# Subtracting the softmax row maxima with 32-row matmuls, fed by one turning matmul, in a fused attention and expert layer

## The reference

```python
mask = jnp.abs(idx[:, None] - idx[None, :]) <= half          # half = 32
scores = jnp.einsum('bhqd,bhkd->bhqk', Q, K) / SCALE
scores = jnp.where(mask[None, None], scores, -jnp.inf)
attn = jax.nn.softmax(scores, axis=-1)
out = jnp.einsum('bhqk,bhkd->bhqd', attn, V)
...
x = x + ga * attention(h)
h = layernorm(x) * (1 + cb) + sb
x = x + gb * experts(h)
```

## Time and profile before

| | |
|---|---|
| median of 3 runs | 164.77 us (163.94 to 164.79) |
| the profiled execution | 163.83 us, of which span 162.0 us |
| TensorE busy | 151.1 us, 93% |
| VectorE busy | 127.1 us, 78% |
| ScalarE busy | 90.2 us, 56% |
| GpSimd busy | 55.9 us, 34% |
| TensorE clock granted | 1.0 of full |
| HBM | 3.81 MB read, 2.10 MB written, mean 36 GB/s |

### The profile page before, as it was taken

One profiled execution on the slowest core, in us unless ns is written; L12 is line 12 of the kernel. 1 busy time (PEld: TensorE's weight loads), 2 busy tenths in 40 slices (PEclk: granted clock), 3 DMA queues, 4 the chain that ended last, 5 costly groups with the idle time before them and its releaser, 6 DMA issues.

```text
span 162.0 us, 5111 instructions
## 1 busy us (share of the span) xinstructions
PE 151.1 (93%) x1976; PEld 123.2 (76%) x1976; DVE 127.1 (78%) x353; ACT 90.2 (56%) x172; POOL 55.9 (34%) x109
## 2 busy tenths in 40 slices
PE   6799989999899999999999999999999999888993
PEld 2376778787677898978887888789888986674773
DVE  3439496495988999897999789877988898587872
ACT  3234387556666656575747764785166428624740
POOL 6420072021540606521662147212251306426340
PEclk9999999999999999999999999999999999999999
DMA  4874134034103503510351013401250000010002
GB/s 134 239 210 28 8 38 32 4 65 28 10 0 46 59 0 67 37 34 4 65 33 35 0 35 43 32 0 35 34 36 0 9 28 0 6 32 0 0 4 65
DMA packets 47431, 6.23 MB, mean 38 GB/s; under 512 B 42416, under 2 KB 47024, under 8 KB 47408
## 3 DMA queue, kind: packets, MB, share of 16 engines
q1 hardware_dynamic: 47264, 5.90, 23.4%
q10 hardware_dynamic: 144, 0.00, 0.0%
HBM read 3.81 MB, written 2.10 MB: 36 GB/s over the span
## 4 chain that ended last, share of the span: by engine, by line
PE 71%; issue 9%; ACT 8%; DVE 6%; POOL 4%; POOLq 0%; ACTq 0%; DVEq 0%
PE ps L763 11%; PE ps L797 11%; PE ps L863 10%; PE ps L778 5%; PE ps L856 5%; PE ps L921 3%; PE ps L839 3%; ACT probs L533 3%; PE ps L841 3%; PE ps L840 3%; PE ps L718 3%; PE ps L808 2%; PE ps L740 2%; PE ps L745 2%; PE ps L890 2%
## 5 line engine op out<-in xcount | busy, mean ns | idle before, releaser
L1160 DVE TRANSPOSE_TENSOR_REDUCE blkmax<-ps 128x44 f32<-128x1408 f32 x16 | 26.4, 1648 | 11.7 <-PE ps L770 9.5
L797 PEld LDWEIGHTS ps<-probs,v_bd 128*36 128x36 f32 x640 | 21.5, 113 | 7.4 <-issue 4.7
L533 ACT ACTIVATE probs<-ps 128x704 f32<-128x704 f32 x32 | 23.0, 755 | 6.1 <-PE ps L778 5.6
L797 PE MATMUL ps<-probs,v_bd 128*36 128x96 f32 (+2 forms) x640 | 25.1, 228 | 0.8 <-ACT probs L533 0.5
L359 POOL TENSOR_TENSOR act_w<-act,cw 128x512 f32<-128x512 f32 x15 | 15.7, 1044 | 21.7 <-issue 13.7
L763 PEld LDWEIGHTS ps<-q_sb,k_bd 32*128 32x128 f32 x640 | 19.3, 186 | 4.3 <-issue 2.4
L763 PE MATMUL ps<-q_sb,k_bd 32*128 32x96 f32 (+2 forms) x640 | 21.3, 274 | 0.7 <-ACT probs L533 0.5
L778 PE MATMUL ps<-shift,quad_ones 128*128 128x384 f32 x64 | 16.9, 370 | 0.0
L863 PE MATMUL ps<-wd_sb,act_t 128*128 128x128 f32 x128 | 16.2, 280 | 0.6
L863 PEld LDWEIGHTS ps<-wd_sb,act_t 128*128 128x128 f32 x128 | 15.0, 191 | 2.0 <-ACT act_t L557 1.8
L546 ACT ACTIVATE tanh_g<-ps 128x512 f32<-128x512 f32 x14 | 8.3, 596 | 14.4 <-PE ps L841 14.4
(11 more groups left out here) (108 smaller groups left out, 283.5 us busy)
## 6 DMA issues: line engine op xcount, KB each, us to landing
x_sb<-x SPq DMA_DIRECT2D x8, 128.0 KB, 3.2
v_spill<-v_sb SPq DMA_DIRECT2D x8, 128.0 KB, 2.3
v_bd<-v_spill SPq DMA_DIRECT2D x32, 32.0 KB, 3.1
out<-out_sb SPq DMA_DIRECT2D x7, 128.0 KB, 2.0
wgu_sb<-w_gu SPq DMA_DIRECT2D x1, 512.0 KB, 4.3
wm_sb<-wmod SPq DMA_DIRECT2D x1, 256.0 KB, 3.8
wd_sb<-w_down SPq DMA_DIRECT2D x1, 256.0 KB, 5.2
con<-consts SPq DMA_DIRECT2D x1, 244.0 KB, 3.2
```

Source lines behind the costliest of these rows:

```text
L533: nc.scalar.activation(probs[:, t, hgs, cols], ps[:, hgs, cols], ACT.Exp, scale=float(DH) ** -0.5).then_inc(probs_ready, 1)
L797: last = nc.tensor.matmul(ps[p0:p0 + VW, OB, c0 + lo * KB:c0 + (hi + 1) * KB], v_bd[:, i % VB, kb, hg, :], view(probs[:, t, hg, at:at + 1] ...
L1160: nc.vector.tensor_reduce(blkmax[:, t, :, live(t):live(t) + LIVE], view(ps[:, 0, live(t) * KB:live(t) * KB + 1], [[BANK, NHG], [KB, LIVE], ...
```

## The change

`shift_rows` for two head groups at a time is replaced by three operations for all four head groups of a half. `spread_max` (VectorE) writes `max_by_head`, in which a column stands for one head group, head and query block, and is nonzero only on the partitions of that head. `turn_max` (TensorE) multiplies it as stationary tile by stacked 32x32 identities and puts the sums into 32 free columns of PSUM bank 0, with head group, head and query block on the partition (`hg*KB + g*QBT + qb`, 16 of each 32 in use) and the query along the columns. `shift_rows` (VectorE) multiplies those by `C_QB`, a negative selector of the query block, into `shift`, 128 partitions x 128 columns. `subtract_max` then contracts over the 32 rows of one head group, with `head_ones`. The subtraction is still four matmuls of 384 columns for a half; each now reads 32 rows, not 128. Both pairs wait for the one shift. The turn and the spread are put at places in the hand-written orders; nothing else is moved.

```diff
-    c[:, C_NI:C_NI + KB] = np.where(r[:, None] == q[None], -1.0, 0.0)
-    c[:, C_ONES:C_ONES + 128] = g[:, None] == g[None]
+    c[:, C_ONES:C_ONES + 128] = (r // QBT)[:, None] == g[None]
...
+    c[:, C_QB:C_QB + QBT] = np.where((r % QBT)[:, None] == np.arange(QBT)[None], -1.0, 0.0)
...
+            def turn_max(i, t):
+                wait(pe, spread_ready, i, QT, t + 1)
+                nc.tensor.matmul(ps[:, 0, CELLS * KB:(CELLS + 1) * KB], max_by_head[:].rearrange("p h m -> p (h m)"),
+                                 con[:, C_REP:C_REP + KB], start=False, stop=True, skip_group_check=True)\
+                  .then_inc(turned_ps, 1)
+
             def subtract_max(i, t, pair):
-                wait(pe, shift_ready, i, PARTS, t * NPAIR + pair + 1)
+                wait(pe, shift_ready, i, QT, t + 1)
                 for hg in range(pair * PAIR, (pair + 1) * PAIR):
-                    last = nc.tensor.matmul(ps[:, hg, 0:CELLS * KB], quad_ones[:],
-                                            view(shift[:, hg, 0:1], [[0, 3], [1, QBT * KB]]),
+                    rows = slice(hg * KB, (hg + 1) * KB)
+                    last = nc.tensor.matmul(ps[:, hg, 0:CELLS * KB], head_ones[rows],
+                                            view(shift[rows, 0, 0:1], [[0, 3], [1, QBT * KB]]),
                                             start=False, stop=True, skip_group_check=True)
...
-            def shift_rows(i, t, pair):
+            def spread_max(i, t):
 
                 wait(dve, rowmax_ready, i, QT, t + 1)
+                wait(dve, turned_ps, i, QT, t)
...
+                nc.vector.tensor_tensor(
+                    view(max_by_head[:, 0, 0:1], [[KB, NHG], [QBT, G], [1, QBT]]),
+                    view(row_max[:, 0, 0:1], [[QBT, NHG], [0, G], [1, QBT]]),
+                    view(con[:, C_DEN:C_DEN + 1], [[0, NHG], [1, G], [0, QBT]]), ALU.mult).then_inc(spread_ready, 1)
+
+            def shift_rows(i, t):
+
+                wait(dve, turned_ps, i, QT, t + 1)
                 wait(dve, shifted_ps, i, PARTS, t * NPAIR)
                 nc.vector.tensor_tensor(
-                    shift[:, pair * PAIR:(pair + 1) * PAIR].rearrange("p h (q k) -> p (h q) k", k=KB),
-                    view(row_max[:, pair * PAIR, 0:1], [[1, PAIR * QBT], [0, KB]]),
-                    view(con[:, C_NI:C_NI + 1], [[0, PAIR * QBT], [1, KB]]), ALU.mult).then_inc(shift_ready, 1)
+                    shift[:], view(ps[:, 0, CELLS * KB:CELLS * KB + 1], [[0, QBT], [1, KB]]),
+                    view(con[:, C_QB:C_QB + 1], [[1, QBT], [0, KB]]), ALU.mult).then_inc(shift_ready, 1)
...
 # TensorE's step(i), images 3 to 5
                 down(i - 3, 1)
+                turn_max(i, 0)
                 transpose_on(i - 1)
...
                 up(i - 2, 1)
+                turn_max(i, 1)
                 logits(i - 1)
```

More of the change, by code:

```diff
@@ L73 @@
 C_HEAD = C_DEN + G
-C_END = C_HEAD + G
+C_QB = C_HEAD + G
+C_END = C_QB + QBT
 def constants():
@@ L160, in program @@
         row_max = sb("row_max", [128, NHG, QBT])
-        shift = sb("shift", [128, NHG, QBT * KB], F32R)
+        max_by_head = sb("max_by_head", [128, NHG, KB])
+        shift = sb("shift", [128, QBT, KB], F32R)
         probs = sb("probs", [128, QT, NHG, CELLS * KB])
@@ L927, in first_step @@
                 keep_clock(3, W1)
+                turn_max(0, 0)
                 project_v(1)
@@ L940, in first_step @@
                 project_k(1)
+                turn_max(0, 1)
                 gates_part(1)
@@ L950, in second_step @@
                 weigh_values(0, 1, 1)
+                turn_max(1, 0)
                 weigh_values(0, 0, 1)
@@ L962, in second_step @@
                 weigh_values(1, 0, 1)
+                turn_max(1, 1)
                 project_k(2)
@@ L974, in third_step @@
                 logits(0)
+                turn_max(2, 0)
                 up(0, 0)
@@ L986, in third_step @@
                 transpose_x1(1)
+                turn_max(2, 1)
                 weigh_values(2, 0, 1)
@@ L1003, in seventh_step @@
                 down(B - 5, 0)
+                turn_max(B - 2, 0)
                 down(B - 5, 1)
@@ L1014, in seventh_step @@
                 weigh_values(B - 2, 0, 0)
+                turn_max(B - 2, 1)
                 up(B - 4, 1)
@@ L1025, in last_step @@
             def last_step():
+                turn_max(B - 1, 0)
                 logits(B - 3)
@@ L1038, in last_step @@
                 weigh_values(B - 1, 0, 1)
+                turn_max(B - 1, 1)
                 output_projection(B - 2)
@@ L1167, in row_maximum @@
                 wait(dve, blkmax_ready, i, QT, t + 1)
-                wait(dve, shift_ready, i, PARTS, t * NPAIR)
+                wait(dve, spread_ready, i, QT, t)
                 nc.vector.tensor_reduce(
@@ L1357, in first_step @@
                 row_maximum(0, 0)
-                shift_rows(0, 0, 0)
-                shift_rows(0, 0, 1)
+                spread_max(0, 0)
+                shift_rows(0, 0)
                 finish_modulation()
@@ L1363, in first_step @@
                 row_maximum(0, 1)
-                shift_rows(0, 1, 0)
-                shift_rows(0, 1, 1)
+                spread_max(0, 1)
+                shift_rows(0, 1)
                 keep_k(1)
@@ L1373, in second_step @@
                 row_maximum(1, 0)
-                shift_rows(1, 0, 0)
-                shift_rows(1, 0, 1)
+                spread_max(1, 0)
+                shift_rows(1, 0)
                 normalise_o(0)
@@ L1379, in second_step @@
                 row_maximum(1, 1)
-                shift_rows(1, 1, 0)
-                shift_rows(1, 1, 1)
+                spread_max(1, 1)
+                shift_rows(1, 1)
                 norm2(0)
@@ L1390, in third_step @@
                 route_compare(0)
-                shift_rows(2, 0, 0)
-                shift_rows(2, 0, 1)
+                spread_max(2, 0)
+                shift_rows(2, 0)
                 normalise_o(1)
@@ L1400, in third_step @@
                 row_maximum(2, 1)
-                shift_rows(2, 1, 0)
-                shift_rows(2, 1, 1)
+                spread_max(2, 1)
+                shift_rows(2, 1)
                 gate(0, 1)
@@ L1491, in step @@
                 row_maximum(i, 1)
-                shift_rows(i, 1, 0)
-                shift_rows(i, 1, 1)
+                spread_max(i, 1)
+                shift_rows(i, 1)
                 gate(i - 2, 1)
```

33 lines of the change are left out of this document (18 added, 15 removed).

## The result

The changed kernel took 183.99 us (median of 4 runs, 182.87 to 185.72) against 164.78 (163.94 to 166.20) before: the ratio is 1.118, 95% interval 1.112 to 1.124. The forecast was 175.8 in a range of 170.0 to 178.5: the sign was right, the size 8 us too small. The profiled execution took 183.17 us, span 181.4. (Single runs disturbed by the chip's slower state are left out of ratios.)

The account below looks back on a forecast made before the run. The prediction took TensorE's queue to bound the kernel (busy 93% of the span). Lags at eleven places summed to 12.0 us, added to the profiled 163.8 us for 175.8, range 170.0 to 178.5.

Parts of the forecast that it names:

- the places: Eleven spots, by image and half, where turn or subtraction makes TensorE's later work late; lags summed to 12.0 us.
- the tail: Image 7, second half: both pairs need the one late shift, delaying up and the drain; +2.1 us.
- place 7: Steps of images 3, 4 and 5, called alike, no turn waiting; 0.8 us each, +2.4 us.
- A lone pair: Two 32-row subtraction matmuls between full-array matmuls: 0.53 us with mode changes, 0.35 before, losing 0.18.
- The visit of four: Four 32-row subtraction matmuls together: 0.53 us with mode changes, 0.71 before, gaining 0.18.
- the way in: TensorE's change from full-array to 32-row matmuls, priced at about 0.15 us, taken as 0.16.
- What would show it: Profile signs listed ahead: idle time at turns, dearer lone pairs, middle steps 17.6 us apart, lower TensorE share, less VectorE work.
- place 8: Image 6, first half: turn between the two downs waits for the spread, second down 1.09 late; +0.9 us.
- Lags absorbed: Rival: half of the 8.8 us of waits is lost because later work waited anyway; 171.4 us, chance 0.18.
- Free mode changes: Rival: going to and from 32-row matmuls costs nothing, about 5 us less; 171 us, chance 0.10.
- No overlap: Rival: the 32-row subtraction matmuls run one behind another, mode changes on top; 182 us, chance 0.08.
- Not slower: Rival: relieved VectorE keeps turns from holding TensorE, the four matmuls overlap without mode cost; 159.0 us, chance 0.04.

Follow-up runs that it names:

- e1: Changed kernel with filler matmuls in the waits ahead of the turns of images 0, 1 and 2, no wait shortened; 177.96 us, ratio 1.084.
- b1: Kernel before, with up(0, 0) of the third step only made to wait for the first shift of image 2; 166.91 us, ratio 1.020.
- b2: b1 with nine filler matmuls in the wait ahead of up(0, 0); 166.33 us, ratio 1.011.
- b3: Kernel before, each subtraction matmul reading 32 rows of the old shift, no turn or new wait, output not the reference's; 165.85 us, ratio 1.012.
- e4: e2 with three turns of images 6 and 7 also moved behind other work and two shifts moved on VectorE; 171.23 us, ratio 1.044.
- e5: Kernel before with 16 unread matmuls of the turn's form added, one ahead of each first subtraction, nothing waiting for them; 167.56 us, ratio 1.019.
- e7: e4 with lone visits of the subtraction put beside another visit of 32 rows; 171.27 us, ratio 1.042.
- e2: Changed kernel with the turns of images 0, 1 and 2 given work ahead or data earlier by moving operations on TensorE and VectorE; 175.55 us, 1.072.
- e3: Changed kernel with the subtraction over all 128 rows, by zero-padded tiles, turns and waits unchanged; 180.12 us, ratio 1.091.
- e9: e1 without the nine fillers of image 2; 179.53 us, ratio 1.093.
- e6: Changed kernel with VectorE's last shift (image 7, second half) moved ahead of residual and norm2; 180.89 us, ratio 1.098.

## Why the prediction was right in sign and short in size

**The step that failed** is the summing of the places with every matmul at its duration of before. The prediction lists lags of 0.8 to 2.1 us where TensorE waits and prices each by its length, with durations from a trace in which the clock was 1.0 throughout. It never asks what an idle stretch does to the matmuls behind it. e1 shows it: same turns, same visits, waits filled, 6 us less. b1 against b2 shows it in the kernel before, where one low stretch cost 1.5 us. The clock took 6.4 of the 19.4 us.

**The places** held. At clock 1.0 the cumulated lag was, forecast and then measured (e1 less its 1.0): (0,1) 1.2, 1.3; (1,0) 1.5, 1.8; (1,1) 3.0, 3.4; (2,1) 4.8, 5.3; (3,0) 5.15, 5.5; (6,0) 7.55, 8.3; (7,0) 8.95, 10.0; (7,1) 9.85, 11.0; and the tail 2.1, 2.0. The largest single miss is place 7: 18.0 us for the step of image 3 and 17.6 for the other two, 2.8 in all for a forecast of 2.4. In image 3's step the prediction's "no turn waits" failed: on the chain of the changed kernel the first turn there follows VectorE's spread and takes 0.41 us, where the later middle steps have 0.14.

```profile
72.02 0.41 PE ps L779 x2
```

By the prediction's own sum the margin there was nearly nothing: in the kernel before, the maximum of that half ends at 59.69 us, the spread would be ready at 59.98, and TensorE reaches the turn's place at 60.02. The three middle steps were called alike, and this one has no row of its own.

**The prices.** A turn on the chain: 0.14 to 0.24 us for a forecast of 0.24, and 3.0 / 16 = 0.19 over the whole kernel. A lone pair: 0.37 + 0.20 = 0.57 against 0.53. The prediction took the pace of the turn's two instructions as that of `down` with its 128 columns, 0.12 us each, and said that it doesn't rest on columns; the 0.14 for both on the chain, and the mean of 0.19, are less with 32 columns. The visit of four, where TensorE goes on with other work behind it (image 6):

```profile
126.38 0.38 PE ps L787 x4
...
126.77 0.47 PE ps L848
```

That is 0.38 us, and 0.23 more on the matmul behind it than the usual 0.24: 0.61 for 0.71 before, a gain of 0.1 where 0.18 was forecast. Less 0.16 for the way in, 0.22 would be streaming (an estimate), against 0.17 taken. The packing gain of the Trainium skill ("TensorE: Matmul & The Clock Gate", Measured speedup vs the span model), from which the prediction worked out 0.23, fits that. Up to the exponential, in the second half of a middle step, the visit of four takes 0.46 us and the pair of the kernel before 0.47, so there it gives nothing, as forecast. Spread 232 ns for 0.22 us, shift 288 ns for 0.29.

**What would show it.** L779 idle 6.7 us on the matmul side, in six waits, for "some 7" in "7 or 8"; longest near image 2's `up`; the pair and the matmul behind it as said; steps 17.6 apart as said; VectorE 4.6 us less busy for "some 5"; the first exponential 1.8 us later (15.32 to 17.09). TensorE's share fell as said (93% to 89%); of the 10.5 us that its busy time rose, the 5.4 of the low clock are what the forecast has no term for. Where the prediction names `down(1, 1)` at place 8, the order has `down(3, 1)`; the times it reads there are right.

**The rivals.** Lags absorbed (171.4) is refuted by the table of starts: none was. Free mode changes (171) by b3 and by the 0.64 and 0.43 us behind lone pairs. No overlap (182) comes close to the time for the wrong reason: a visit of four took 0.38 on TensorE and not 0.71. Not slower (159.0) names relief of VectorE as its cause; that relief came, and e4, with the turns moved and the clock full, is still at 1.044. There the profile counts 6.3 us from the first scores to the end: 3.0 for turns (e5), 1.0 for visits (b3), and 2.3 that no run isolated; the waits that are left may be in them, which is argued and not shown.

**What stays open** is what sets the length of a low stretch, and why one came in b3 and e7 with next to no wait. The runs give 3.4 us (b1, b3, e7, the tail of e1 and e2, and image 0 of the changed kernel), 6.8 (e3, and e9 in two pieces), 10.2 (e6 from 15.1 us) and 13.7 (the changed kernel and e6 round image 2). Nor does the length of a wait settle whether one comes: the 1.50 us ahead of the last shift's subtraction were followed by a fall in e1 and e2, and by none in the changed kernel and e9. The Trainium skill ("TensorE: Matmul & The Clock Gate", A second HAM failure mode) tells of a kernel whose short idle pieces between groups of matmuls were frequent enough to swing the clock between its levels; b3 would fit that. The profile of the kernel before has the same pieces and no fall, yet 4 of the 42 runs of it beside the experiments have a mean clock of 0.99 and take 164.7 to 164.9 us; of b3 5 of 6 runs have 0.99. A mean of 0.99 is one stretch of 3.4 us, so the kernel before has one too, rarely, and b3 mostly; where, in the runs without a profile, isn't known.

## What to carry to other kernels

A new wait on TensorE is priced twice: by its length, and by what the matmuls behind it cost if the granted clock falls to half (6.4 us here); so look at the granted clock in the profile, and put movable or filler work into the wait. An operand sent round through a second engine and back makes that engine's result due earlier by a round trip; place the round trip's first half behind work that needs nothing of it (here 12.8 of 19.2 us), and don't expect savings ahead of it to be kept in full (e7). A tidier operand (32 rows for 128) was no gain in this queue of full-array matmuls: changing the mode cost 0.2 us for each lone pair, and a visit of four gained 0.1 in the queue and nothing ahead of an exponential.

## What was not expected of the hardware

The clock first rises at a different moment from run to run, with the same instructions ahead of it. In the kernel before it was full by 8.1 us; in b2 it was not until 13.2. Durations show it: the view by windows gives 1.00 for the time ahead of a trace's first clock record, in b2 too. The same two matmuls of `project_k`, of the kernel before and then of b2:

```profile
8.09 0.67 PE L735 MATMUL ps<-h_t,wqkv_sb 128*128 128x256 f32 x2 [0.63 <-ACT h_t L475]
```

```profile
8.34 1.19 PE L735 MATMUL ps<-h_t,wqkv_sb 128*128 128x256 f32 x2 [0.20 <-ACT h_t L475]
```

That moves the first scores from 10.3 to 12.0 us and all behind them, which is as much as some of the effects studied here; so kernels were compared from their first scores as well as by their whole time.
